# Making the score of tile n+3 before the weighing of tile n+2 on VectorE, in the head pairs of a graph attention kernel

## The reference

```python
def gat_conv(x, src, dst, W, a_src, a_dst, b):
    h = (x @ W).reshape(N, H, C)              # N=1250, H=4 heads, C=192
    as_n = (h * a_src).sum(-1)
    ad_n = (h * a_dst).sum(-1)
    e = leaky_relu(as_n[src] + ad_n[dst], 0.2)
    m = segment_max(e, dst, num_segments=N)
    p = exp(e - m[dst])
    s = segment_sum(p, dst, num_segments=N)
    alpha = p / (s[dst] + 1e-16)
    out = segment_sum(alpha[:, :, None] * h[src], dst, num_segments=N)
    return out.reshape(N, H * C) + b
x1 = relu(layernorm(x) @ W_ah + b_ah)
xs = [relu(gat_conv(x1, src, dst, W, a_s, a_d, b)) for the 3 layers]
return relu(concatenate(xs, axis=1) @ W_out + b_out)
```

## Time and profile before

| | us |
|---|---|
| median of 3 runs | 1500.35 |
| lowest and highest run | 1499.09, 1502.5 |
| profiled execution, its own time | 1500.28 |
| span of its instructions | 1498.5 |
| PE matmul busy | 1394.9 (93%) |
| PE weight load busy | 1290.7 (86%) |
| DVE busy | 1065.4 (71%) |
| ACT busy | 468.5 (31%) |
| mean granted TensorE clock | 0.966 |

### The profile page before, as it was taken

One profiled execution on the slowest core, in us unless ns is written; L12 is line 12 of the kernel. 1 busy time (PEld: TensorE's weight loads), 2 busy tenths in 40 slices (PEclk: granted clock), 3 DMA queues, 4 the chain that ended last, 5 costly groups with the idle time before them and its releaser, 6 DMA issues.

```text
span 1498.5 us, 21123 instructions
## 1 busy us (share of the span) xinstructions
PE 1394.9 (93%) x8180; PEld 1290.7 (86%) x8180; DVE 1065.4 (71%) x1950; ACT 468.5 (31%) x782; POOL 36.5 (2%) x41
## 2 busy tenths in 40 slices
PE   4999899899999697979999999999999999997788
PEld 4965566899999697979999999999999999997654
DVE  6858988699999532576776677577667767675554
ACT  3210122334443401434333432342343334222140
POOL 2100000000000040000000000000000000000000
PEclk9999999999999798999999999999999999999995
DMA  8310000212220475400201110120111011022003
GB/s 244 130 64 0 2 1 1 84 67 84 84 84 35 139 227 171 120 35 0 72 1 67 35 37 1 67 72 1 67 35 38 1 67 40 1 81 72 1 0 103
DMA packets 23300, 90.99 MB, mean 61 GB/s; under 512 B 3549, under 2 KB 4800, under 8 KB 20269
## 3 DMA queue, kind: packets, MB, share of 16 engines
q1 hardware_dynamic: 22289, 87.47, 17.9%
q10 hardware_dynamic: 924, 2.30, 0.6%
HBM read 78.70 MB, written 11.06 MB: 60 GB/s over the span
## 4 chain that ended last, share of the span: by engine, by line
PE 50%; DVE 8%; ACT 3%; issue 1%; DVEq 0%
PE psum L1514 21%; PE psum L101 8%; PE psum L102 8%; PE psum L103 8%; DVE prob L1232 2%; DVE prob L1226 2%; PE psum L1597 2%; ACT prob L1387 2%; DVE hN L1246 1%; PE psum L1528 1%; PE psum L1565 1%; PE psum L1577 1%; DVE acc L1268 1%; DVE xll L1259 0%; DVE x1l L1253 0%
## 5 line engine op out<-in xcount | busy, mean ns | idle before, releaser
L1514 PE MATMUL psum<-hN,prob 125*125 125x193 f32 x2400 | 411.5, 328 | 12.4 <-DVE hN L1246 7.6
L1514 PEld LDWEIGHTS psum<-hN,prob 125*125 125x125 f32 x2400 | 396.7, 188 | 14.0 <-issue 10.8
L1387 ACT ACTIVATE prob<-prob,acol 125x1250 f32<-125x1250 f32 x120 | 160.9, 1341 | 396.9 <-DVE prob L1226 396.8
L1232 DVE SCALAR_TENSOR_TENSOR prob<-prob,cnt 125x1250 f32<-125x1250 f32 x120 | 174.8, 1457 | 80.3 <-ACT prob L1387 80.3
L1226 DVE SCALAR_TENSOR_TENSOR prob<-vrow,ncol,urow 125x1250 f32<-125x1250 f32 x120 | 181.9, 1516 | 0.0
L704 DVE CUSTOM_DVE_ANT_0 junk<-mask,arow 125x1250 bf16<-125x1250 uint8 x120 | 174.8, 1457 | 3.1
L101 PE MATMUL psum<-woh,xlh 128*125 128x384 f32 x360 | 128.9, 358 | 15.7 <-DVE acc L1268 15.7
L101 PE MATMUL psum<-wph,x1h 128*125 128x384 f32 x330 | 118.9, 360 | 8.8 <-DVE x1l L1253 8.8
L102 PE MATMUL psum<-wol,xlh 128*125 128x384 f32 x360 | 124.3, 345 | 0.0
L103 PE MATMUL psum<-woh,xll 128*125 128x384 f32 x360 | 123.6, 343 | 0.0
L596 PE MATMUL psum<-hot_src,hot_dst 125*125 125x416 bf16 (+1 forms) x588 | 115.8, 352 | 8.1 <-DVE hot_src L426 8.1
(11 more groups left out here) (210 smaller groups left out, 2206.6 us busy)
## 6 DMA issues: line engine op xcount, KB each, us to landing
arow<-scratch_a SPq DMA_DIRECT2D x12, 625.0 KB, 3.9
urow<-scratch_uv SPq DMA_DIRECT2D x12, 625.0 KB, 4.0
vrow<-scratch_uv SPq DMA_DIRECT2D x12, 625.0 KB, 5.9
wq_raw<-in_w_qkv SPq DMA_DIRECT2D x6, 1152.0 KB, 6.6
wp_raw<-in_w_pair SPq DMA_DIRECT2D x6, 1152.0 KB, 7.4
wo_raw<-in_w_out SPq DMA_DIRECT2D x6, 1152.0 KB, 5.9
wl<-in_w_gat SPq DMA_DIRECT2D x4, 1152.0 KB, 7.0
xN<-in_x SPq DMA_DIRECT2D x10, 336.0 KB
```

The lines of the kernel that those rows point to most:

```text
L1232: nc.vector.scalar_tensor_tensor(prob[n % RING][:, :], prob[n % RING][:, :], 1.0, cnt[:, n % NT, :], op0=ALU.min, op1=ALU.mult).then_inc(p ...
L1387: nc.scalar.activation(prob[n % RING][:, :], prob[n % RING][:, :], ACT.Exp, bias=acol[:, n // NT, n % NT:n % NT + 1]).then_inc(e_ready, 1)
L1514: last = nc.tensor.matmul(bank(t // 2)[0:P, 193 * (t % 2):193 * (t % 2) + 193], ring[:, t * P:(t + 1) * P], hN[i % 2][:, j, 193 * s:193 * ...
```

## The change

In every iteration of DVE's loop, `scores(tile + AHEAD)` moves from behind `accumulate`, `statistics` and `layer_norm` to the front, ahead of `weigh(tile + AHEAD - 1)`. Nothing is added or taken out; the waits inside the two functions stay as they are, and the other engines' programs are the same.

```diff
@@ -1351,6 +1351,8 @@
                         scale_up()
                     if tile + AHEAD == 0:
                         residual_stored()
+                    if 0 <= tile + AHEAD < ALL:
+                        scores(tile + AHEAD)
                     if 0 <= tile + AHEAD - 1 < ALL:
                         weigh(tile + AHEAD - 1)
                     if i + 1 < PAIRS and n >= NT:
@@ -1363,8 +1365,6 @@
                         statistics(n - 2)
                     if i == PAIRS and 3 <= n < NT + 3:
                         layer_norm(n - 3)
-                    if 0 <= tile + AHEAD < ALL:
-                        scores(tile + AHEAD)
                     if 0 <= i < PAIRS and n % NT == NT - 1:
                         normalise(i, n // NT)
                     if 1 <= i < PAIRS and n < NT:
```

## The result

The changed kernel takes 1502.99 us (median of 22 runs, 1499.5 to 1505.8) against 1500.39 before (22 runs, 1496.5 to 1502.5): ratio 1.0019, 95% interval 1.0012 to 1.0026. It is 2.6 us slower. That is less than the 3.0 which the prediction took for no change, but the interval is clear of 1, the sign is the other than in the forecast of 1.9 faster, and the time lies 0.5 above the upper end of the range. The profiled execution took 1499.5, the fastest of its runs; a second one, taken later, took 1504.76.

The account below looks back on a forecast made before the run. PE, 93% busy, was taken as the bound, with DVE edits gaining only where PE waits. Terms 9.27 - 5.72 - 1.76 + 1.57 - 1.5 = 1.86 faster gave 1498.4 us, range 1495.0 to 1502.5.

Parts of the forecast that it names:

- The start: Ahead of pair 0 and in its first head: aggregations begin earlier and stop waiting for weighings, gain 9.27 us.
- its price on the clock: Pair 0, behind PE's idle gap of 2.8 before `hidden`: lower clock costs 0 to 3 us, taken as 1.5.
- The changes of heads: Pairs 1 to 4: the score ahead of the weighing delays accumulate and PE's `outputs` by 1.43 us, four times, loss 5.72.
- the weights: Pairs 1 to 4, behind the next pair's weights' subtraction: accumulate later, PE loses 0.44 us, four times, 1.76.
- The end: Pair 5: `outputs` starts later, but nine aggregations then run back to back without waiting for weighings, gain 1.57 us.
- Rival (3): Changes of heads: four waits grow from 0.40 to 1.83, clock falls, 1.5 each; 4.1 us slower, 1504.4; chance 0.13.
- scatter of the tail: Forecast case's own scatter, some 1.5 us either way, since the tail's clock phases shift with its start.

Follow-up runs that it names:

- The kernel early at the start alone: Kernel before, with the score early only ahead of pair 0 and in its first head: 1490.34 us, ratio 0.9926.
- The changed order with two exceptions in twenty iterations and one swap: Changed kernel with the score back in its old place at n = 10 and n = 6, accumulate ahead of x1_low at n = 10: 1481.94 us, ratio 0.9869.

## Why the prediction was wrong

Taken from the first `hidden` of pair 0, which stood at 589.18 before and at 590.08 and 591.00 in the two executions of the changed kernel, the steps compare so:

| step | forecast | measured |
|---|---|---|
| first `hidden` to the first aggregation of the second head, pair 0 | 70.2 | 69.7, 70.2 |
| to `hidden` of pair 1 | 76.4 | 75.9, 76.4 |
| fall of the clock behind that gap | 1.5 | 1.54 (665.98 to the next aggregation at 670.75 is 4.77, before 3.23) |
| PE's delay at a change of heads, pairs 1 to 4 | 1.43 each | 1.43 each |
| PE's delay behind the next pair's weights | 0.44 each | 0.43 each |
| falls of the clock behind the waits of 1.83 | none | 2 and 3 of 4, at 1.53 |
| to the last pair's first transposes | 779.3 | 781.8, 783.8 |

- **The start** was right, and so was its price on the clock, though that price was an estimate from one row. The moved score in front of `x1_low` opened a gap of 2.70 (2.8 forecast), and the clock fell behind it in all five executions that had that gap. The kernel early at the start alone shows the gain by itself.
- **The changes of heads and the weights** were right to 0.01. The wait of 0.40 was no slack but the sign that none was left. The moved score was again a step of 1.43 (794.39 to 795.82). The weights' loss is in the rows:

```profile
766.41 1.51 DVE L1226 SCALAR_TENSOR_TENSOR prob<-vrow,ncol,urow 125x1250 f32<-125x1250 f32 x1
767.85 1.45 DVE L1232 SCALAR_TENSOR_TENSOR prob<-prob,cnt 125x1250 f32<-125x1250 f32 x1
769.22 1.01 DVE L1268 TENSOR_TENSOR acc<-acc,psum 125x384 f32<-125x384 f32 x2
```
```profile
769.91 0.41 PE L101 MATMUL psum<-woh,xlh 128*125 128x384 f32 x1 [0.19 <-DVE acc L1268]
```

- **The end** was right: the last nine aggregations run in one piece, and no weighing is late.

```profile
1341.35 29.57 PE L1514 MATMUL psum<-hN,prob 125*125 125x193 f32 x180
```

- **What failed** is the term that the sum does not have: it puts the clock behind the four waits of 1.83 at nothing. Rival (3) had the mechanism and the price (1.5) right, and also that more than one fall of the four decides against the change, but I gave it 0.13. The reasons were the gaps of 1.22 and 1.73 in the earlier trace rows, which had left the clock up, and that PE is fully busy on both sides. What the runs showed in its place: of twelve waits of 1.83, seven brought the clock down, at 1.53 each, and with them filled none did. Waits of 1.72 to 1.74 left it up in all of the seven places where the traces have them in the six pairs, so the row of 1.73 was read rightly; what did not hold was that 1.83 would do the same. The trace of before had the witness. In its tail PE waits eight times for accumulate; behind the four waits of 1.71 the clock stayed up, and behind two of the four of 1.82 it fell:

```profile
1405.93:1409.93 4.00, 4.00 (x15) 4.00 (x16) 3.21 (x7) 0.29 (x1) 0.00 (x0) 0.63 0.00 0
1413.65:1417.65 4.00, 4.00 (x14) 4.00 (x15) 3.21 (x7) 0.29 (x1) 0.00 (x0) 0.57 0.00 0
```

  The prediction has these falls only as scatter of the tail. With 2.5 falls of 1.53 the forecast would have been 1498.4 + 3.8 = 1502.2, inside the range and 0.8 under the measured 1503.0.
- **The range** took in one or two of four falls and no more. As the waits are alike, their falls should have been one case from none to all four, 0 to 6.1, and the upper end 1504 or 1505. That the median missed the range by only 0.5 is chance: two or three of four places fell in the executions seen, and not four.
- The Trainium skill (TensorE: Matmul & The Clock Gate, section "Why this matters for your kernels") advises against PE-idle gaps between bursts of matmuls, but its limit is above 2.70. Here 2.70 brought the clock down in five of five executions and 1.83 in 7 of 12 places, so the measurement decides against that limit.

Open is the rest of 0.8. Open is also what decides whether the clock falls behind a given wait of 1.8, above all behind the one of 1.84 in the tail, which alone is worth 3.0. The traces show it in one or two executions of each kernel; how often it happens in the other runs is not known. That filling the waits for accumulate keeps the clock up behind them is shown.

## What to carry to other kernels

Moving one instruction forward in an in-order queue moves everything between its old place and its new one back by its length, in every iteration; look for the places where the engine that waits has no slack (here those with a wait already shown) and leave the old order there. The changed order with two exceptions in twenty iterations and one swap gave 19 us, where the same move made everywhere lost 2.6. A new wait of PE is to be charged with its length and with the clock behind it.

## What the hardware showed

- Behind waits of 1.83 between stretches of full work the granted clock fell from 2.4 to 1.2 GHz in 7 of 12 places; behind 1.21 in none of 4, behind 0.98 in none of the four read in one execution, behind 1.27 in pair 0 in none of five executions, behind 2.70 in five of five.
- In the tails without extra matmuls (twelve executions) it fell behind 19 of 48 waits for accumulate of 1.81 or 1.82, and behind 1 of 48 of 1.71. These waits stand in other surroundings than those of 1.83, so this is no threshold, but a tenth of a microsecond more came with many more falls.
- A fall costs 1.53 in the six pairs, and its mean clock over the 4 us behind it is 0.57 to 0.68. Behind the wait of 1.84 in the tail it costs 3.0 (11.17 against 8.16); it came there in 10 of 14 executions.
- Useless matmuls in the wait keep the clock up: with three in each, the stretch from the first `hidden` to the last transposes took 778.7, against 781.8 and 783.8 without.
- A PE wait shown as 0.40 cost 0.64, and one shown as 0.19 cost 0.43: 0.24 more than shown, both times.
